# Two-layer transformer on one core: keys stored without zero rows, 64-row score products paired by parity, and loops written out

## The chip, the cores and the metric

One core of one Trainium2 chip runs the whole program. The time is device time in microseconds of one execution, from three runs; lower is better. The engines are named as in the profile: PE (TensorE matmul), PEld (its weight loads), DVE (VectorE), ACT (ScalarE), POOL (GpSimd) and SP (SyncE, which issues DMAs here).

## What is computed

A batch of 4 sequences of 512 tokens by 256 channels goes through two layers, each an attention and a feed-forward part with a residual and a layer norm behind both.

```python
x = layernorm(x + attn0(x))   # 16 heads of 16, 4 key heads, rotary, band |i-j| <= 64, sink
x = layernorm(x + ffn0(x))    # silu(x Wg sg) * (x Wu su), then Wd sd, int8 weights, 1024 wide
x = layernorm(x + attn1(x))   # 16 heads of 16, rotary, causal, biases
x = layernorm(x + ffn1(x))    # shared experts plus the 2 best of 16 experts for each token
```

Both attentions are softmax(q k^T / 4) v for each head:

```python
att = einsum('bhqd,bhkd->bhqk', q, k) * hd ** -0.5    # masked
out = einsum('bhqk,bhkd->bhqd', softmax(att), v)
```

## The kernel before, in words

**Phase 1** handles one sequence of the batch at a time: `batch(b, last)` does attention 0, feed-forward 0 and attention 1, on every engine. Sequences 0 to 2 are turns of a loop (`Fori(0, B - 1)`) and sequence 3 (`last`) stands behind it as straight code. **Phase 2** does the expert layer for all tokens: 4 turns of a loop over the shared experts (`Fori(0, B)`), then 47 tiles of 128 gathered tokens through `run_steps`, in which 7 steps are straight code (`PEELED`), 40 are 5 turns of a loop of 8 steps, and 3 more close it. A step transposes one tile (L1530), multiplies an earlier one with its expert's first weights (L1539), transposes the result of one before that (L1547) and multiplies with the second weights (L1556). The expert of a tile is read into a register (L1510).

**Attention.** A head has 16 channels. For a product of float32 quality q and k are stacked in 48 rows of high and low parts, with row 48 for a shift: 64 rows (`STACK`) for a head, two heads in 128 partitions. `stack` makes them in `q_st` and `k_st` (ACT the high parts, DVE the low), `stack_tr` turns them on PE (L1229, L1238), and copies put them into `qT` and `kT`. `qT` holds an even head in partitions 0 to 63 and the odd one beside it in 64 to 127. `kT` has one block of 128 partitions for every head, of which the other head's 64 rows are zero: a memset at the start (L820) zeroes it, DVE's `k_copy` (L882) fills the even blocks' upper half and ACT (L661) the odd blocks' lower half. So every product uses all 128 rows, and the other head's rows of q meet zeros.

The heads go in 4 groups of 4. A group takes three passes, and six **steps** s = 0 to 5 overlap them: step s does the raw products of group s and the scores, exponentials and value products of group s - 2.

- A **raw item** (`raw_item`) is a query tile t with some heads: a mask product on PE (L1283 in layer 0, L1286 in layer 1), then q times k for each head (L1290) into banks 0 to 2; DVE takes the maximum over the keys (L982) as the shift of the softmax. Layer 0 has 8 items of 2 heads in a step; layer 1 has 11 (one of 4 heads, two of 2, eight of 1). A mask product waits until DVE has read the item three before it.
- A **score item** (`score_item`) is a head with one or two key tiles, k times q (L1303) into banks 3 to 5, which ACT exponentiates (L714, L717) and POOL masks (L518). There are 8 of them in a step in layer 0 and 12 in layer 1.
- `pv_part` multiplies with v (L1317), four heads beside each other in four strips of 32 columns of the array.

PE's order in a step is score item i, then raw item i. All orders are the order of the code; semaphores join the engines. In a loop a wait counts against a register made from the turn (`REGISTER_ALU` rows below). `keep_clock` puts idle products (L1179) where PE would wait.

## Time and profile before

| | |
|---|---|
| median of 3 runs | 1138.18 us |
| lowest, highest | 1136.27, 1138.29 us |
| the profiled execution | 1141.58 us |
| its span, first to last instruction | 1139.9 us |
| mean granted TensorE clock | 0.839 |
| PE, DVE, ACT, POOL busy | 846.4, 628.6, 461.8, 370.5 us |
| phase 1, phase 2 (about) | 0 to 838 us, 838 to 1140 us |

The profile gives start and length of every instruction in us from the span's start. On PE the starts are what to go by: the lengths overlap, since matmuls are pipelined. "idle" in square brackets is what the engine stood still before a row, with what ended it; "issue" means that nothing in the profile was waited for.

### The profile page before, as it was taken

To read this page: it belongs to the slowest core of one execution; us is meant where nothing else is said; L and a number is where in the kernel's file an instruction comes from. 1 tells how busy PE (TensorE), PEld (TensorE's weight loads), DVE (VectorE), ACT (ScalarE), POOL (GpSimd) and SP (SyncE) were. 2 spreads that over 40 slices of the span, in tenths; PEclk is the share of its full clock that TensorE was granted. 3 is DMA by queue.
4 is the path that set the end of the run, shared out by engine and by line. 5 is a ranking of instruction groups with operands and counts; after the bars stand their busy time and mean duration, and the time that the engine had idled before them with its cause. 6 is when DMAs were issued, how large, how long until landed. Compare 5 with 4: busy or idle time off the path is not lost.

```text
span 1139.9 us, 17645 instructions
## 1 busy us (share of the span) xinstructions
PE 846.4 (74%) x5446; PEld 646.4 (57%) x5447; DVE 628.6 (55%) x1478; ACT 461.8 (41%) x960; POOL 370.5 (32%) x595
## 2 busy tenths in 40 slices
PE   2497989988888995878899797889820388889600
PEld 1475765667566664757666575765520277777500
DVE  4473478446248745724884653578360055666555
ACT  1554434744543474454347463444510033444300
POOL 5034441412444041244414142431223600122384
PEclk9598979958888998889899897989855588899955
DMA  9300000000000000000000000000069301243233
GB/s 317 115 3 1 20 1 1 2 20 4 1 20 1 1 2 22 3 1 20 1 1 2 20 2 1 1 1 2 1 206 261 150 18 37 84 126 123 88 111 105
DMA packets 34606, 54.04 MB, mean 47 GB/s; under 512 B 4545, under 2 KB 28865, under 8 KB 33657
## 3 DMA queue, kind: packets, MB, share of 16 engines
q0 software_dynamic: 8192, 27.43, 7.7%
q1 hardware_dynamic: 18624, 18.62, 5.9%
q10 hardware_dynamic: 7704, 6.91, 1.9%
q8 instruction: 46, 0.75, 0.3%
q14 instruction: 40, 0.32, 0.1%
HBM read 24.76 MB, written 20.71 MB: 40 GB/s over the span
## 4 chain that ended last, share of the span: by engine, by line
PE 39%; issue 30%; POOL 13%; DVE 10%; ACT 3%; DMA 2%; another core or an unknown queue 1%; POOLq 0%; SPq 0%; DVEq 0%; ACTq 0%
POOL prob L518 5%; PE ps L1303 4%; PE ps L1194 4%; PE ps L1539 4%; PE ps L1317 3%; PE ps L1179 3%; DVE negmax L982 3%; POOL fT L528 3%; PE ps L1290 3%; PE ps L1556 2%; PE ps L1466 2%; POOL back L576 2%; PE ps L1229 2%; DMA x<-in_x 2%; PE ps L1422 2%
## 5 line engine op out<-in xcount | busy, mean ns | idle before, releaser
L982 DVE TENSOR_REDUCE negmax<-ps 128x2 fp32r<-128x512 f32 (+4 forms) x304 | 178.1, 628 | 61.5 <-PE ps L1290 58.8
L1290 PE MATMUL ps<-kT,qT 128*128 128x256 f32 (+4 forms) x512 | 155.3, 382 | 0.0
L1303 PE MATMUL ps<-qT,kT 128*128 128x192 f32 (+4 forms) x512 | 120.6, 322 | 11.9 <-DVE xT L833 5.1
L513 POOL TENSOR_TENSOR carry_p<-neg_half 128x1 f32<-128x1 f32 x80 | 16.5, 207 | 307.6 <-ACT prob L717 161.9
L518 POOL TENSOR_SCALAR_AFFINE_SELECT prob<-prob 128x512 f32<-128x512 f32 (+1 forms) x192 | 109.9, 602 | 0.0
L1303 PEld LDWEIGHTS ps<-qT,kT 128*128 128x128 f32 x512 | 80.1, 191 | 49.0 <-ACT prob L717 24.2
L616 ACT ACTIVATE xT<-ps 128x256 fp32r<-128x256 f32 x100 | 37.3, 383 | 169.4 <-PE ps L1187 168.7
L717 ACT ACTIVATE prob<-ps 128x512 f32<-128x512 f32 (+1 forms) x192 | 89.2, 518 | 37.6 <-PE ps L1303 36.5
L1290 PEld LDWEIGHTS ps<-kT,qT 128*128 128x128 f32 x512 | 99.0, 207 | 3.3
L1317 PE MATMUL ps<-prob,v_aug 128*32 128x256 f32 (+4 forms) x1024 | 77.9, 412 | 13.2 <-POOL prob L518 13.1
L833 DVE TENSOR_TENSOR xT<-ps,xT 128x256 fp32r<-128x256 f32 x100 | 41.3, 421 | 63.7 <-ACT xT L616 63.4
L714 ACT ACTIVATE prob<-ps,sink 128x448 f32<-128x448 f32 x128 | 71.7, 623 | 11.3 <-PE ps L1303 11.3
L493 POOL TENSOR_TENSOR rstd<-mv,neg_half 128x1 f32<-128x1 f32 x48 | 31.6, 657 | 134.0 <-DVE mv L920 134.0
L557 POOL DMA_DIRECT2D slot_y<-ys_sb x47 | 25.5, 543 | 142.8 <-DVE ys_sb L1135 142.5
L1229 PE MATMUL ps<-ident_r,q_st 128*128 128x128 f32 x256 | 46.8, 339 | 29.8 <-DVE q_st L865 17.9
L968 DVE RECIPROCAL rden<-ps 128x16 f32<-128x16 f32 x32 | 8.2, 255 | 108.4 <-PE ps L1328 108.4
L1229 PEld LDWEIGHTS ps<-ident_r,q_st 128*128 128x128 f32 x256 | 42.3, 246 | 37.9 <-DVE q_st L865 14.8
L1283 PE MATMUL ps<-band,ident_b 128*128 128x384 bf16 (+1 forms) x128 | 50.7, 396 | 16.6 <-issue 9.1
L1187 PE MATMUL ps<-ident,x 128*128 128x128 f32 x136 | 28.8, 312 | 45.1 <-DVE x L938 23.9
L1194 PE MATMUL ps<-wqkv_s,xT 128*128 128x512 f32 (+2 forms) x288 | 59.0, 356 | 2.0 <-ACT qkv_sb L630 1.4
L476 POOL TENSOR_TENSOR rot_c<-qkv_sb,rot 128x320 f32<-128x320 f32 (+1 forms) x32 | 37.3, 1167 | 58.1 <-DVE qkv_sb L949 40.4
L528 POOL TENSOR_TENSOR fT<-fuse_sb,fT 128x512 fp32r<-128x512 f32 x32 | 41.1, 1290 | 45.7 <-ACT fT L742 45.7
(180 smaller groups left out, 1852.9 us busy)
## 6 DMA issues: line engine op xcount, KB each, us to landing
slot_x<-zeros ACTq DMA_DIRECT2D x1, 6016.0 KB, 30.5
xs_sb<-slot_x SPq DMA_DIRECT2D x47, 128.0 KB, 2.0
slot_y<-ys_sb POOLq DMA_DIRECT2D x47, 128.0 KB, 2.0
w_sb<-in_w POOLq DMA_DIRECT2D x4, 1408.0 KB
w_sb<-in_w POOLq DMA_DIRECT2D x5, 704.0 KB, 7.9
x<-in_x SPq DMA_DIRECT2D x4, 512.0 KB, 3.6
x_rows<-x SPq DMA_DIRECT2D x4, 512.0 KB, 3.2
x_all<-x_rows SPq DMA_DIRECT2D x1, 2048.0 KB, 30.4
```

The lines of the kernel that those rows point to most:

```text
L518: ins = pool.affine_select(out=sel, in_=sel, compare_op=ALU.is_ge, fill=0.0, base=base, pattern=[[0, GH], [sign, hi_q - lo_q]], channel_mu ...
L528: pool.tensor_tensor(out=fT[:, 1, m, :], in0=fuse_sb[:, m % 2, :], in1=fT[:, 0, m, :].bitcast(F32), op=ALU.subtract).then_inc(f_lo.sem, 1)
L714: act.activation(prob[:, part % PROB_BUFS, j, 0:n], ps[:, 3 + i % 3, 0:n], ACT.Exp, bias=sink4[:, h:h + 1], scale=SCALE).then_inc(exped[l] ...
L717: act.activation(prob[:, part % PROB_BUFS, j, 0:n], ps[:, 3 + i % 3, 0:n], ACT.Exp, scale=SCALE).then_inc(exped[l].sem, 1)
L982: dve.tensor_reduce(out=negmax[:, t, s * GH + j * mh:s * GH + (j + 1) * mh], in_=ps[:, k % 3, 0:mh * n].rearrange("p (h n) -> p h n", n=n) ...
L1194: ins = pe.matmul(dst, xT[:, a, k, t * P:(t + 1) * P], w[:, w_part, k, c0:c0 + n], start=(i + k == 0), stop=(i == 2 and k == KC - 1))
L1229: ins = pe.matmul(ps[:, 2 + n // 4, (n % 4) * P:(n % 4 + 1) * P], q_st[:, 2 * n:2 * n + 2, :].rearrange("p h s -> p (h s)"), ident_r[:], s ...
L1283: pe.matmul(dst, ident_b[:], band[:, m0:m0 + n].unsqueeze(1).to_broadcast([P, mh, n]), start=True, stop=False, skip_group_check=True)
L1290: ins = pe.matmul(dst[:, jj, :], qT[:, h // 2, t * P:(t + 1) * P], kT[:, k_block(h), k0:k0 + n], start=False, stop=True, skip_group_check= ...
L1303: ins = pe.matmul(ps[:, 3 + item % 3, col:col + n], kT[:, k_block(h), kt * P:(kt + 1) * P], qT[:, h // 2, q0:q0 + n], start=True, stop=Tru ...
L1317: ins = pe.matmul(ps[32 * j:32 * j + 32, 6, q0:q0 + n], v_aug[l][:, kt, h // 4 if l == 0 else h, :], prob[:, (g * n_parts + p) % PROB_BUFS ...
L1539: ins = pe.matmul(ps[:, (r - 1) % 2, 0:2 * I], xsT[:, (r - 1) % 2, part, k, :], w13_sb[:, bass.ds(e, 1), k, :], start=(part + k == 0), sto ...
```

## The change

`kT` loses its zero rows: it has 8 blocks instead of 16, the even head in rows 0 to 63, the odd one in 64 to 127, as `qT`. The memset and all of DVE's `k_copy` go; ACT's copy takes all 128 partitions. A raw or score product now takes the 64 rows of its head (`half(h)`); in the built program these are in 64x128 tiles of the array, at row 0 or row 64, while the mask products, the turning products and the transposes keep the full 128x128 array. A raw item has two heads of the same parity, (1,3) then (0,2), or a single one in the order 1, 0, 3, 2, so that layer 1 has 12 items of one or two heads where it had 11; its neighbouring score item has the other parity. In a step that has both, PE's order becomes mask, raw, score, raw, score. All seven loops on each engine are written out as Python loops.

```diff
+def raw_heads(layer, t):
+    if 2 * query_tile_keys(layer, t)[1] <= 512:
+        return [(1, 3), (0, 2)]
+    return [(1,), (0,), (3,), (2,)]
...
-        kT = sb("kT", [P, H, T], F32R)
+        kT = sb("kT", [P, PAIRS, T], F32R)
...
-    with eng.Fori(0, STEP_TURNS) as m:
+    for m in range(STEP_TURNS):
...
-            with pe.Fori(0, B - 1) as b:
+            for b in range(B - 1):
                 batch(b, False)
...
-                act.activation(kT[STACK:P, 1:2 * n_blk:2, t * P:(t + 1) * P],
-                               ps[STACK:P, K_BANK[l]:K_BANK[l] + 2, :]
+                act.activation(kT[:, 0:n_blk, t * P:(t + 1) * P],
+                               ps[:, K_BANK[l]:K_BANK[l] + 2, :]
...
-            dve.memset(kT[:].bitcast(F32), 0.0).then_inc(start_dve.sem, 1)
...
-            def k_copy(b, l, t):
-                n_blk = (KVH0, PAIRS)[l]
-                dve.wait_ge(*k_tr[l].at(b, t + 1))
-                dve.tensor_copy(kT[0:STACK, 0:2 * n_blk:2, t * P:(t + 1) * P],
...
+                    def half(h):
+                        return slice(STACK * (h % 2), STACK * (h % 2) + STACK)
...
-                            ins = pe.matmul(dst[:, jj, :], qT[:, h // 2, t * P:(t + 1) * P], kT[:, k_block(h), k0:k0 + n],
+                        ins = pe.matmul(raw_dst(g, i)[:, a, :], qT[half(h), h // 2, t * P:(t + 1) * P],
+                                        kT[half(h), k_block(h), k0:k0 + n], start=False, stop=True, skip_group_check=True)
...
-                        for i in range(max(n_items, n_parts * GH)):
-                            if g >= 0 and i < n_parts * GH:
-                                score_item(g, i)
-                            if s < NG and i < n_items:
-                                raw_item(s, i)
+                        for i in range(n_items):
+                            if raws:
+                                raw_mask(s, i)
+                            if scores:
+                                score_free(g, i)
+                            for a in range(2):
+                                if a < raws:
+                                    raw_head(s, i, a)
+                                if a < scores:
+                                    score_tile(g, i, a)
```

How PE's order moves in step 2 of layer 1's attention, items 2 to 4 (L1286 is the mask product, L1290 a raw product, L1303 a score product). Before:

```order
L1303 MATMUL ps<-qT,kT 128x512
L1276 REGISTER_ALU
L1286 MATMUL ps<-causal_q,ident_b 128x128
L1290 MATMUL ps<-kT,qT 128x384
L1300 REGISTER_ALU
L1303 MATMUL ps<-qT,kT 128x384
L1303 MATMUL ps<-qT,kT 128x128
```

The same place in the changed kernel (L1284 mask, L1292 raw, L1310 score, L1350 the turning of the maxima):

```order
L1284 MATMUL ps<-causal_q,ident_b 128x2x128
L1292 MATMUL ps<-kT,qT 128x256
L1310 MATMUL ps<-qT,kT 128x512
L1292 MATMUL ps<-kT,qT 128x256
L1284 MATMUL ps<-causal_q,ident_b 128x128
L1292 MATMUL ps<-kT,qT 128x384
L1310 MATMUL ps<-qT,kT 128x384
L1310 MATMUL ps<-qT,kT 128x128
```

The score now follows a raw product of the other half instead of leading the item, and the register rows are gone.

PE in the expert steps, at the head of a turn of the loop before (L1510 reads the experts, ISA rows put the address into the matmul):

```order
L1510 TENSOR_LOAD owner
L1510 ISA x2
L1534 REGISTER_ALU
L1536 REGISTER_ALU
L1539 ISA
L1539 MATMUL ps<-w13_sb,xsT 128x352
L1539 ISA
L1539 MATMUL ps<-w13_sb,xsT 128x352 x3
L1545 REGISTER_ALU
L1547 MATMUL ps<-ident,h_sb 88x128 x2
L1510 ISA
L1510 TENSOR_LOAD owner
```

In the changed kernel all 40 steps have this form, which is also that of the later straight steps before:

```order
L1524 TENSOR_LOAD owner
L1524 ISA x2
L1553 ISA
L1553 MATMUL ps<-w13_sb,xsT 128x352
L1553 ISA
L1553 MATMUL ps<-w13_sb,xsT 128x352 x3
L1561 MATMUL ps<-ident,h_sb 88x128 x2
L1570 ISA
L1570 MATMUL ps<-w2_sb,hT 128x256
```

The second read of an expert, which the first two steps of every turn had, and the register rows are gone.

## Rows read from the trace of the kernel before

**Rows 1.** The page: the span, and the chain that ended last by engine.

```profile
span 1139.9 us, 17645 instructions
PE 39%; issue 30%; POOL 13%; DVE 10%; ACT 3%; DMA 2%; another core or an unknown queue 1%; POOLq 0%; SPq 0%; DVEq 0%; ACTq 0%
```

**Rows 2.** Windows on single steps: length, busy us and instructions by engine, clock, DMA.

```profile
core 0: us, PE busy (x) PEld busy (x) DVE busy (x) ACT busy (x) POOL busy (x), PEclk, DMA share, GB/s
469.90:475.60 5.70, 5.70 (x44) 5.28 (x45) 4.16 (x7) 4.48 (x9) 1.43 (x4) 1.00 0.01 3
475.60:483.80 8.20, 8.20 (x81) 6.51 (x80) 5.26 (x10) 5.95 (x12) 5.51 (x12) 1.00 0.01 3
...
582.50:588.30 5.80, 5.39 (x31) 3.22 (x32) 5.80 (x11) 0.59 (x1) 0.00 (x0) 1.00 0.01 4
588.30:596.40 8.10, 8.07 (x56) 5.40 (x55) 7.21 (x13) 5.47 (x12) 2.15 (x5) 1.00 0.00 1
596.40:607.10 10.70, 10.59 (x86) 6.74 (x84) 6.90 (x11) 6.76 (x15) 2.92 (x7) 1.00 0.01 2
```

**Rows 3.** Timeline of PE, layer 0: items in steps 3 and 0, and around `pv_part`.

```profile
475.87 0.34 PE L1283 MATMUL ps<-band,ident_b 128*128 128x384 bf16 x1
...
476.50 0.34 PE L1283 MATMUL ps<-band,ident_b 128*128 128x384 bf16 x1
...
476.76 0.27 PE L1290 MATMUL ps<-kT,qT 128*128 128x192 f32 x1
476.96 0.37 PE L1317 MATMUL ps<-prob,v_aug 128*32 128x192 f32 x4
...
477.53 0.39 PE L1317 MATMUL ps<-prob,v_aug 128*32 128x256 f32 x3
477.86 0.36 PE L1303 MATMUL ps<-qT,kT 128*128 128x192 f32 x1
...
651.42 0.39 PE L1283 MATMUL ps<-band,ident_b 128*128 128x512 bf16 x1
...
651.89 0.39 PE L1283 MATMUL ps<-band,ident_b 128*128 128x512 bf16 x1
```

**Rows 4.** Windows on step 0 of layer 0 in sequences 2 and 3.

```profile
455.45:463.69 8.24, 6.08 (x28) 5.05 (x29) 4.49 (x8) 0.02 (x1) 0.00 (x0) 0.59 0.02 5
...
650.21:654.46 4.25, 4.19 (x29) 3.49 (x29) 3.69 (x7) 0.02 (x1) 0.00 (x0) 1.00 0.00 0
```

**Rows 5.** Timeline of PE where sequences 1, 2 and 3 begin.

```profile
256.78 0.48 PE L1283 MATMUL ps<-band,ident_b 128*128 128x384 bf16 x1 [1.68 <-issue]
...
265.25 0.33 PE L1283 MATMUL ps<-band,ident_b 128*128 128x384 bf16 x1
...
455.45 0.32 PE L1283 MATMUL ps<-band,ident_b 128*128 128x384 bf16 x1 [3.82 <-issue]
...
458.68 0.61 PE L1283 MATMUL ps<-band,ident_b 128*128 128x512 bf16 x1 [2.15 <-issue]
...
650.21 0.32 PE L1283 MATMUL ps<-band,ident_b 128*128 128x384 bf16 x1 [0.60 <-ACT kT L661]
```

**Rows 6.** Timeline of PE in the expert steps, straight and looped.

```profile
983.58 0.38 PE L1530 MATMUL ps<-ident,xs_sb 128*128 128x128 f32 x2
...
986.87 0.38 PE L1530 MATMUL ps<-ident,xs_sb 128*128 128x128 f32 x2
...
1007.43 0.91 PE L1539 MATMUL ps<-w_sb,xsT 128*128 x4 [0.68 <-issue]
...
1024.44 0.91 PE L1539 MATMUL ps<-w_sb,xsT 128*128 x4 [0.71 <-issue]
```

**Rows 7.** Timeline of PE and DVE around the last `stack_tr` of sequence 3.

```profile
647.20 1.08 PE L1229 MATMUL ps<-ident_r,q_st 128*128 128x128 f32 x8 [1.00 <-ACT qT L657]
...
648.77 0.68 DVE L882 CAST kT<-ps 64x512 fp32r<-64x512 f32 x1 [1.52 <-PE ps L1238]
```

**Rows 8.** Timeline of ACT in the first turn of the shared experts.

```profile
901.94 0.32 ACT L786 ACTIVATE act_a<-ps 128x176 f32<-128x176 f32 x1 [7.37 <-issue]
```

More of the change, by code:

```diff
@@ L407, in _ @@
                 load(q, q)
-            with sp.Fori(0, (NS - 4) // 4) as m:
+            for m in range((NS - 4) // 4):
                 for r in range(4):
@@ L533, in _ @@
                 head_step(0, k)
-            with pool.Fori(0, B - 1) as b:
+            for b in range(B - 1):
                 batch(b, False)
@@ L560, in _ @@
                 store(q, q)
-            with pool.Fori(0, (NS - 3) // 4) as m:
+            for m in range((NS - 3) // 4):
                 for i in range(4):
@@ L762, in _ @@
             act.activation(gw_s[:, 0, :, :], gw_raw[:], ACT.Copy).then_inc(gw_split.sem, 1)
-            with act.Fori(0, B - 1) as b:
+            for b in range(B - 1):
                 batch(b, False)
@@ L774, in _ @@
             load_table(2, ACT.Silu)
-            with act.Fori(0, B) as b:
+            for b in range(B):
                 for t in range(NT):
@@ L931, in norm @@
                             split_lo(b, ("x1", "x2")[i], t)
-                    if i == 2 and not last:
-                        k_copy(b + 1, 0, NT - 1)
                 def scale_tile(i, t, result):
@@ L1025, in _ @@
                               op=ALU.subtract).then_inc(gw_split.sem, 1)
-            with dve.Fori(0, B - 1) as b:
+            for b in range(B - 1):
                 batch(b, False)
@@ L1090, in _ @@
             dve.wait_ge(x3_back.sem, 16)
-            with dve.Fori(0, B) as b:
+            for b in range(B):
                 for t in range(NT):
@@ L1434, in _ @@
             pe.wait_ge(gw_split.sem, 2)
[L1435 removed]
+            for b in range(B - 1):
                 batch(b, False)
@@ L1450, in _ @@
             pe.wait_ge(shared_in.sem, 32)
-            with pe.Fori(0, B) as b:
+            for b in range(B):
                 pe.wait_ge(*xg_in.at(b, 16))
```

89 lines of the change are left out of this document (44 added, 45 removed).

## The prediction

> **What bounds the kernel now.** I first read the page's chain. Its largest share after PE is "issue", time in which an engine waited for nothing that the profile shows, a third of it [rows 1]. So the question is what PE does where it is the last to come, and two places matter here: the scoring steps of both attentions, which are about 100 of the 200 us of a sequence, and the expert steps of phase 2.
>
> Second, windows cut at the first product of a step. Steps with scores and raws are long and PE is busy all through them ([rows 2], the first two and the last two), with DVE and ACT at 5 to 7 us of the same window. In layer 1 a step with raw products alone takes 5.80 us, and DVE's 11 maxima fill all of it ([rows 2], third): there PE may be slower without anyone noticing, up to a point. In layer 0 such a step takes 4.25 us at the full clock ([rows 4], second).
>
> Third, the timeline of PE gives what one item costs. A raw item of 512 mask columns and two products of 256 takes 0.47 us from mask to mask ([rows 3], last two), 0.61 ns for a column. An item with scores in layer 0 takes 0.63 us from mask to mask ([rows 3], first two): 384 mask columns, 0.16 us at 2.4 columns a ns, and four products in the other 0.47 us, so 0.12 us each.
>
> Fourth, the places where a loop turns [rows 5, 6].
>
> **The loops written out.** *Expert steps.* A row that comes once in a turn of 8 steps comes again after 17.01 us ([rows 6], last two); I looked at four such rows and they are all 17.0 us apart. In front of it PE stands for 0.7 us with nothing to wait for. The straight steps ahead of the loop, which already carry all four stages, take (986.87 - 983.58) / 2 = 1.645 us ([rows 6], first two). The order of the changed kernel shows the 40 looped steps in just that form: no register arithmetic, no second read of an expert. 8 x 1.645 = 13.2 us for a turn, so 3.85 us less, and 5 x 3.85 = **-19.3 us**. What could come late then: SP's loads and POOL's stores, one each for a step; in the straight steps they kept up. Bounds: 0 if the straight steps owe their speed to loads that were made ahead, -21 if all goes as in the best of them.
>
> *Between sequences.* Sequence 3 follows without a jump: PE starts it 0.60 us after its idle products, when ACT's copy is there, and has done step 0 after 4.25 us. Sequence 2 starts after 3.82 us for no reason shown, stands again for 2.15 us, falls to a mean granted clock of 0.59 and needs 8.24 us for the same step [rows 4, 5]. That is 3.2 + 4.0 = 7.2 us. Sequence 1: 1.68 - 0.60 = 1.1 us and 265.25 - 256.78 - 4.25 = 4.2 us, together 5.3. The stops look like code that has to be read again after the jump. Sum **-12.5 us**; the lower bound, if the clock stays low there anyway, is the stops alone, about -7.
>
> *Shared experts.* Their turns follow each other through data, so I take nothing. There is one unknown: in the first turn ACT stands for 7.37 us with nothing to wait for [rows 8], while the experts' weights come in. The same code is read there after the change. It may go either way by a few us; I take 0.
>
> **The copies.** DVE loses `k_copy`, 0.68 us in layer 0 [rows 7]. But PE's start of the next turning product waits for ACT's copy of q, and DVE stands for 1.52 us before its copy [rows 7]: ACT's copies and PE's products are the loop there, and ACT's copy keeps its length, for it has the same columns in more partitions. The memset at the start lies under the first loads. I take **0**; the bound is one copy a sequence, -3 us in all.
>
> **The scoring steps.** No 64-row tile is in the trace. The nearest is the one other place where PE changes the shape of its tiles, from 128x128 to strips of 128x32 and back [rows 3]. From the last full product to the first strip it is 0.20 us where products otherwise follow after 0.12: 0.08 us of standstill. And the first product behind a change is 0.36 us long where its like is 0.27: 0.09 us, in which its weights are loaded, that are otherwise loaded under the product before. So a change costs up to 0.17 us. The changed kernel changes twice for each raw item, since masks stay at 128 rows and the products are at 64. For the way back, to the mask, whose bf16 weights load faster, I take half of the second part less: 0.26 us an item in all, between 0 (rows of a tile may change freely) and 0.34.
>
> The page "TensorEngine Tiling (Array Packing)" of the Trainium skill says in its section "Key Properties" that a change of the tiling mode, not of the tile alone, drains TensorE. By that rule each mask of this kernel costs two drains; the rows on the strips agree with it, and no row here shows it for a change of rows.
>
> Against that stands the pairing. A raw product and the score behind it are in different halves, write different banks, and may run together. The four strip products start within 0.02 us of each other: 0.37 us for four [rows 3]. So for a pair I take one product's time.
>
> - Layer 0, step 0: 8 raw items of 0.42 us (0.47 and, by the same ns a column, 0.35 to 0.37 for the narrow ones) plus 0.26: 5.4 us against 4.25, **+1.2**. Step 1 has 6.2 us of other work on DVE, and hides it: 0.
> - Layer 0, steps 2 and 3: per item + 0.26 - 2 x 0.12 = 0.02, so +0.15 a step, **+0.3**.
> - Layer 1, steps 0 and 1: by 0.61 ns a column the 12 items are 2 x 0.31 + 2 x 0.47 + 4 x 0.31 + 4 x 0.39 = 4.4 us, plus 12 x 0.26 = 3.1: 7.5 us against 5.80, so DVE's cover is gone, +1.7 each, **+3.4**. DVE's twelfth maximum is covered then.
> - Layer 1, steps 2 and 3: + 3.1 us of changes, less what pairs hide: 0.21 for a 512-column score under the two raws of an item, 0.16 for 384 columns, 0.12 for 256, four items each, 2.0 us. PE has +1.1 us, of which I let half go into the waits for ACT and DVE that these steps have: **+1.1** for both. Bounds: 0 and 2.2.
> - Steps 4 and 5 have no masks, change no more often than before, and are ACT's: 0.
>
> Sum 6.0 us a sequence, **+24 us**. A hundredth of a us in the cost of an item is some 0.6 us a sequence where PE leads, so 2.4 us in all.
>
> Last, the new order puts a mask's wait for DVE ahead of the score that stood before it. Queued behind it are the score, and with it ACT. With three banks ahead this seldom binds in steps 2 and 3, where DVE is busy 7 of 8 to 10 us; I take 0, and at most 0.2 us a step.
>
> **Sum.** 1138.2 - 19.3 - 12.5 + 24.0 = **1130 us**. On the profiled execution, 1141.58 us with a span of 1139.9, the same terms give 1133.8; it lies 3.4 us above the median of the runs.
>
> **Rivals.**
> (a) *Changing rows is free and pairs overlap.* Then steps 0 and 1 stay DVE's, step 2 of layer 0 ACT's, and the gain is in step 3 of layer 0, 8 x 0.24 = 1.9 us of which 1.5 count, and in steps 2 and 3 of layer 1, 2.0 us of work each of which 0.5 and 1.5 count: 3.5 us a sequence, -14. 1138.2 - 31.8 - 14 = **1092 us**. For it speaks that the rows on the change are of columns, not of rows; against it, that both directions of that change cost. The Trainium skill's page "TensorE: Matmul & The Clock Gate", section "Part 3: Packing small matmuls", has row tiles run side by side, four of them 3.07 times as fast as one after another; no row here shows it.
> (b) *Free, but the pairs don't overlap*: the scoring stays, **1106 us**.
> (c) *Slower: the changes cost and the pairs don't overlap*, because the weights of a pair are loaded one after another. A product of 192 columns needs 0.08 us at 2.4 columns a ns but takes 0.12, so loading bounds layer 0's items already. Then steps 2 and 3 cost 8 x 0.26 = 2.1 us each in layer 0, and 3.1 less 1 us of waits in layer 1: 1.2 + 4.2 + 3.4 + 4.2 = 13 us a sequence, +52: **1158 us**. In general the kernel gets slower when the scoring costs over 8 us a sequence, that is at 0.29 us an item by my sum.
> (d) *Writing out the expert loop gives nothing*, as code must be brought for every step: -19.3 is gone, **1150 us**. Against it stand the straight steps.
>
> **How the numbers follow.** Forecast 0.43, (a) 0.22, (b) 0.10, (c) 0.18, (d) 0.07. The forecast's own range, by 0.20 to 0.31 us an item, is 1115 to 1143; two thirds of it are below 1136. The range goes to (a), and towards (c) without reaching it: 1093 to 1153. A measurement of this kernel can tell about 0.2% from no change. Faster: 0.22 + 0.10 + 0.29 = 0.61; same: 0.08; slower: 0.31.
>
> **What would show it.** In the expert steps the transposes (L1530 before) must come 1.6 to 1.7 us apart throughout. Sequences 1 and 2 must start like sequence 3, without "issue" of 2 to 4 us. In layer 1 step 0, the window must grow from 5.80 to about 7.5 us with DVE no longer busy throughout, and the first raw product behind a mask must start 0.1 us or more after the mask's columns are through; if it starts 0.04 us behind the mask as before and the window stays at 5.8, (a) or (b) holds. Whether a raw product and the score behind it start within 0.02 us of each other tells (a) and the forecast from (b) and (c). My sum is wrong from the ground if the first turn of the shared experts grows or shrinks by over 10 us, or if the clock in the scoring steps falls with the standstills.

## The result, and the profile after

| | before | after |
|---|---|---|
| median | 1137.22 us (1134.86 to 1138.29) | 1269.76 us (1261.04 to 1276.79) |
| span of the profiled execution | 1139.9 us | 1264.2 us |
| mean granted TensorE clock | 0.839 | 0.734 |

The changed kernel takes 1.1165 times as long (95% interval 1.1085 to 1.1244): 132 us slower, where 8 us less was forecast, and far beyond the range of 1093 to 1153 us.

The page of the changed kernel; the rows that answer to [rows 1], and the granted clock in 40 slices of the span (tenths):

```profile
span 1264.2 us, 15264 instructions
...
PEclk9556976687678757978875896697576565789955
...
PE 68%; DVE 10%; ACT 5%; POOL 5%; DMA 5%; issue 4%; another core or an unknown queue 2%; ACTq 0%; DVEq 0%; SPq 0%; POOLq 0%
```

"issue" fell from 30% to 4% of the chain, and PE took its place and more. It is 4% too in the kernel with the loops alone written out (below), which gains 1%: a large share of the chain under "issue" was not time to be won.

Windows on the steps of sequence 2, cut at the first product of a step: steps 0 to 3 of layer 1, then steps 0 to 3 of layer 0. The columns are those of [rows 2]; the last but two is the granted clock.

```profile
core 0: us, PE busy (x) PEld busy (x) DVE busy (x) ACT busy (x) POOL busy (x), PEclk, DMA share, GB/s
646.05:653.55 7.50, 7.50 (x29) 3.88 (x27) 6.16 (x11) 0.00 (x0) 0.00 (x0) 0.90 0.00 0
653.55:665.08 11.53, 11.53 (x33) 5.88 (x32) 7.23 (x12) 0.59 (x1) 0.00 (x0) 0.50 0.00 1
665.08:679.14 14.06, 14.06 (x57) 6.95 (x56) 7.22 (x12) 6.29 (x12) 2.14 (x5) 0.50 0.01 2
679.14:696.65 17.51, 17.51 (x85) 8.55 (x86) 7.00 (x12) 7.27 (x14) 2.91 (x7) 0.50 0.01 1
517.75:523.88 6.13, 6.13 (x29) 3.51 (x28) 4.91 (x8) 0.13 (x1) 0.00 (x0) 1.00 0.01 3
523.88:531.47 7.59, 6.54 (x34) 3.75 (x32) 6.34 (x13) 1.86 (x5) 0.00 (x0) 1.00 0.00 1
531.47:540.70 9.23, 9.23 (x45) 4.82 (x44) 4.45 (x8) 5.00 (x8) 2.32 (x5) 0.56 0.00 1
540.70:551.39 10.69, 10.69 (x82) 5.52 (x82) 5.55 (x10) 6.53 (x11) 4.63 (x10) 0.74 0.01 2
```

This is the whole finding in eight rows. Layer 1's steps 1, 2 and 3 took 5.80, 8.10 and 10.70 us at 1.00 before [rows 2], and step 0 took 5.80 us as well:

```profile
576.70:582.50 5.80, 5.30 (x28) 2.87 (x26) 4.99 (x10) 0.00 (x0) 0.00 (x0) 1.00 0.00 0
```

After, step 0 takes 7.50 us and is nearly through when the clock drops; steps 1 to 3 run at 0.50, that is at 1.2 instead of 2.4 GHz, and PE is busy all through them. DVE and ACT, with 7 us of work each, are no bound any more. In layer 0 the clock holds for two steps and drops in the third.

Timeline of PE in layer 0: an item of step 0, then a paired item of step 3, both at the full clock.

```profile
518.28 0.34 PE L1281 MATMUL ps<-band,ident_b 128*128 128x384 bf16 x1
518.54 0.47 PE L1292 MATMUL ps<-kT,qT 64*128 64x192 f32 x2
518.94 0.39 PE L1281 MATMUL ps<-band,ident_b 128*128 128x512 bf16 x1
...
549.35 0.34 PE L1281 MATMUL ps<-band,ident_b 128*128 128x384 bf16 x1
549.62 0.35 PE L1292 MATMUL ps<-kT,qT 64*128 64x192 f32 x1
549.62 0.38 PE L1310 MATMUL ps<-qT,kT 64*128 64x256 f32 x1
...
550.02 0.34 PE L1281 MATMUL ps<-band,ident_b 128*128 128x384 bf16 x1
```

A raw product and its score start together (549.62 twice), so pairs overlap. The first raw product starts 0.26 to 0.27 us behind a mask whose 384 columns need 0.16 us, so 0.10 us is a standstill; the rest of what the item grew by stands between its products and the next mask. An item takes 0.67 us where it took 0.63 [rows 3].

Two neighbouring expert steps, and the longest stop of ACT in the first turn of the shared experts (the places of [rows 6, 8]):

```profile
1139.79 0.38 PE L1544 MATMUL ps<-ident,xs_sb 128*128 128x128 f32 x2
...
1141.45 0.38 PE L1544 MATMUL ps<-ident,xs_sb 128*128 128x128 f32 x2
...
1054.94 0.32 ACT L791 ACTIVATE act_a<-ps 128x176 f32<-128x176 f32 x1 [12.22 <-remote]
```

Put together from the two traces, span against span (+124.3 us): the scoring of layer 0, from the first mask product to the last transpose of a sequence, went from 188.5 to 243.0 us over the four sequences, +54.5; layer 1's from 209.7 to 301.0, +91.3; the rest of phase 1 is 16.2 us shorter; the routing and the end give 5.5 us back; the shared experts went from 87.2 to 102.5, +15.3; the expert steps from 95.4 to 80.3, -15.1.

### The profile page after: what moved, and what is told of

Same layout as the page of the kernel before. It is cut to its first block, busy times and chain, and to the rows that moved or that the text cites. A ratio compares the mean times of both kernels' runs of the same rounds, so it can differ in the third digit from the quotient of the medians.

```text
span 1264.2 us, 15264 instructions
## 1 busy us (share of the span) xinstructions
PE 991.3 (78%) x5462; PEld 668.5 (53%) x5462; DVE 608.4 (48%) x1461; ACT 468.0 (37%) x960; POOL 367.8 (29%) x595
## 4 chain that ended last, share of the span: by engine, by line
PE 68%; DVE 10%; ACT 5%; POOL 5%; DMA 5%; issue 4%; another core or an unknown queue 2%; ACTq 0%; DVEq 0%; SPq 0%; POOLq 0%
PE ps L1292 13%; PE ps L1325 7%; PE ps L1428 5%; PE ps L1310 5%; PE ps L1184 4%; PE ps L1281 4%; PE ps L1284 4%; DMA xg<-x_rows 4%; PE ps L1169 3%; PE ps L1553 3%; PE ps L1219 3%; PE ps L1177 3%; POOL back L582 2%; PE ps L1480 2%
## 5 line engine op out<-in xcount | busy, mean ns | idle before, releaser
L974 DVE TENSOR_REDUCE negmax<-ps 128x2 fp32r<-128x512 f32 (+4 forms) x320 | 193.5, 610 | 186.2 <-PE ps L1292 181.6
L1292 PE MATMUL ps<-kT,qT 64*128 64x256 f32 (+4 forms) x512 | 212.2, 483 | 0.0
L1310 PE MATMUL ps<-qT,kT 64*128 64x256 f32 (+4 forms) x512 | 168.1, 466 | 6.3 <-ACT prob L720 4.9
L1292 PEld LDWEIGHTS ps<-kT,qT 64*128 64x128 f32 x512 | 114.3, 261 | 66.2 <-issue 49.1
L723 ACT ACTIVATE prob<-ps 128x512 f32<-128x512 f32 (+1 forms) x192 | 94.2, 522 | 97.1 <-PE ps L1310 96.5
L1325 PE MATMUL ps<-prob,v_aug 128*32 128x256 f32 (+4 forms) x1024 | 108.7, 549 | 9.7 <-POOL prob L524 9.6
L1310 PEld LDWEIGHTS ps<-qT,kT 64*128 64x128 f32 x512 | 95.0, 259 | 38.4 <-ACT prob L723 14.1
L1281 PE MATMUL ps<-band,ident_b 128*128 128x384 bf16 (+1 forms) x128 | 59.8, 467 | 10.2 <-DVE gw_s L1014 5.2
L1284 PE MATMUL ps<-causal_q,ident_b 128*128 128x128 bf16 (+1 forms) x192 | 59.3, 309 | 0.0
L1325 PEld LDWEIGHTS ps<-prob,v_aug 128*32 128x32 f32 x1024 | 31.0, 135 | 49.8 <-issue 26.1
```

The source lines that it names most:

```text
L723: act.activation(prob[:, part % PROB_BUFS, j, 0:n], ps[:, 3 + i % 3, 0:n], ACT.Exp, scale=SCALE).then_inc(exped[l].sem, 1)
L974: dve.tensor_reduce(out=negmax[:, t, s * GH + heads[0]:s * GH + heads[-1] + 1:2], in_=ps[:, k % 3, 0:mh * n].rearrange("p (h n) -> p h n", ...
L1281: pe.matmul(dst, ident_b[:], band[:, m0:m0 + n].unsqueeze(1).to_broadcast([P, mh, n]), start=True, stop=False, skip_group_check=True)
L1284: pe.matmul(dst[:, :, n - P:n], ident_b[:], causal_q[:].unsqueeze(1).to_broadcast([P, mh, P]), start=True, stop=False, skip_group_check=True)
L1292: ins = pe.matmul(raw_dst(g, i)[:, a, :], qT[half(h), h // 2, t * P:(t + 1) * P], kT[half(h), k_block(h), k0:k0 + n], start=False, stop=Tr ...
L1310: ins = pe.matmul(ps[:, 3 + item % 3, col:col + n], kT[half(h), k_block(h), kt * P:(kt + 1) * P], qT[half(h), h // 2, q0:q0 + n], start=Tr ...
```

## The experiments

All times come with the ratio to the kernel before on the same chip. The kernels on one line of thought stand together.

| kernel | median us | ratio to before (95%) |
|---|---|---|
| only the loops written out | 1129.8 | 0.9907 (0.9863 to 0.9952) |
| changed kernel, but full rows | 1109.3 | 0.9726 (0.9701 to 0.9751) |
| the same, shared experts a loop again | 1098.5 | 0.9654 (0.9605 to 0.9703) |
| changed kernel, pairs taken apart | 1401.6 | 1.2146 (1.2054 to 1.2238) |
| changed kernel without masks | 1130.7 | 0.9921 (0.9873 to 0.9969) |
| full rows without masks | 1111.2 | 0.9784 (0.9718 to 0.9851) |
| full rows, masks in column strips | 1240.0 (1201.7 to 1246.9) | no interval |
| changed kernel, masks twice | 1260.3 (1237.2 to 1278.6) | no interval |
| masks twice in layer 0, four times in layer 1 | 1255.0 | 1.0997 (1.0899 to 1.1094) |

The kernels with stops inside their items have wide times, since layer 0 of one and the same code is found at either level of the clock (below). Their medians are read loosely, and their steps closely. The traces read are of one execution each: 1415.8 us of the kernel with pairs taken apart, 1242.3 with strips (the fastest took 1201.7), 1257.4 with masks twice, and 1294.7 with masks two and four times, the longest of its five.

### Which part of the change costs

**Only the loops.** The kernel before with `for ... in range` for every `Fori`.

> The kernel before with all its loops written out and nothing else changed. By my sum the expert steps give 19.3 us and the starts of sequences 1 and 2 give 12.5 us: 1137 - 32 = 1105 us. Two readings differ. (1) The written-out loops are good by themselves and all of the loss is in the scoring: 1105 us, each sequence about 200 us, shared experts 141 us as before. (2) The written-out code costs something where the changed kernel lost 22 us in the shared experts: then this kernel shows 160 us there too, and about 1125 us in all. In both the granted clock is 1.00 in the scoring steps of layer 1.

Measured 1129.8 us: a gain of 1%, some 10 us, a third of the 32 us. The clock stayed at 1.00 in layer 1's scoring and the steps kept their length. The expert steps took 79.8 instead of 95.4 us (-15.6), the routing begins 8 us earlier, but the shared experts took 99.5 instead of 87.2 us. Reading (2).

**Full rows.** The changed kernel with this taken back, and with it the memset, DVE's copies and the numbering of the blocks:

```diff
-        kT = sb("kT", [P, PAIRS, T], F32R)
+        kT = sb("kT", [P, H, T], F32R)
...
-qT[half(h), h // 2, t * P:(t + 1) * P], kT[half(h), k_block(h), k0:k0 + n]
+qT[:, h // 2, t * P:(t + 1) * P], kT[:, k_block(h), k0:k0 + n]
```

> The changed kernel with one thing taken back: keys keep their zero rows, so that raw and score products use the full 128x128 array (with DVE's copies and the memset that belong to it). The new order mask, raw, score, raw, score, the items of one parity, the twelfth item of layer 1 and the written-out loops stay. (Half) If the 64-row tiles are the cause, by their effect on the clock or by their switches, the granted clock stays 1.00 in the scoring steps, and the time is that of the kernel with only the loops written out, within 6 us. (Order) If the new order is the cause, in which a mask's wait for DVE stands ahead of the score and so ahead of ACT, PE shows stops before the masks and the time stays over 1200 us.

Measured 1109.3 us. The clock is back, with the new order, the twelve items and the loops in place (layer 1 of sequence 2, steps 2 and 3):

```profile
567.70:575.50 7.80, 7.80 (x56) 5.44 (x56) 6.69 (x13) 5.56 (x12) 2.15 (x5) 1.00 0.02 4
575.50:585.45 9.95, 9.95 (x86) 6.63 (x85) 6.74 (x13) 6.78 (x15) 2.92 (x7) 1.00 0.01 2
```

So the 64-row tiles cost 160 us, and the order costs nothing. It even gains: this kernel is 20 us below the one with loops alone, outside the 6 us that I had allowed. These two steps took 8.20 and 10.60 us there, 0.40 and 0.65 us more. Between the two traces, whose executions are 12.8 us apart, the scorings of all sequences are 11.7 us shorter; 2.8 us of that are step 0 of layer 0, which was entered at a higher clock. Where the rest of the 20 us comes from is not settled.

**Pairs taken apart.** The changed kernel with the score item ahead of the mask:

```diff
-                            for a in range(2):
-                                if a < raws:
-                                    raw_head(s, i, a)
-                                if a < scores:
-                                    score_tile(g, i, a)
+                            for a in range(scores): score_tile(g, i, a)
+                            raw_mask(s, i)
+                            for a in range(raws): raw_head(s, i, a)
```

> The changed kernel with 64-row products, but in the old order: both products of a score item, then the mask, then both raw products, so that neighbouring products are hardly ever in opposite halves. Two switches of the tile shape for each raw item stay. It tells what the pairing gives. The changed kernel hides one product of 0.12 us (0.2 at half clock) behind another for each pair: 16 pairs a step in layer 0, 16 to 24 in layer 1. If the pairs were worth their full time, this kernel takes 8 x 2 x 0.12 to 0.2 = 2 to 3 us more in each of the four steps with raws and scores, 8 to 12 us a sequence and 32 to 48 us in all: 1300 to 1318 us. (Activity) If the clock follows how busy the array is, the standstills in a longer step lower it further or no less, and layer 1 stays at 0.50. (Pairs worthless) the same 1270 us.

Measured 1401.6 us, 132 us above the changed kernel, three times what I expected. At half the clock every product that isn't hidden counts double: steps 2 and 3 of layer 1, at 0.50 in both kernels, took 18.56 and 22.7 us instead of 14.06 and 17.51. In layer 0 the same two steps took 13.7 us and some 16 at 0.50, where those of the changed kernel took 10.0 and some 12 when they ran at 0.50. That is about 17 us a sequence, some 70 us in all, for the pairing. Another 30 us are not the pairing's: layer 0 ran at the lower level from its step 0 on (10.4 us instead of 6.1, and 12.7 instead of 7.6). The pairing works, as forecast; it cannot pay for what makes it possible.

### Standstills or half rows

**Masks left out.** Both kernels leave out the mask products of the raw items; the maxima then cover masked keys too.

> The changed kernel without its mask products (the first raw product starts the bank instead; the maxima then cover masked keys too, which the output doesn't show where no exponential underflows). So the scoring steps have 64-row products, pairs and all, but no change of the tile shape inside an item; what changes is left to the value products and the transposes of the shifts. It is to be read against the same kernel with full rows, which has no masks either. (Standstills) If the clock falls because of the stops at the changes of shape, it stays at 1.00 here in layer 1's scoring, and pairing can pay for the first time: layer 0 steps 2 and 3 and layer 1 steps 2 and 3 get shorter than with full rows by some 2 x 0.8 and 2 x 1 us, and the time is at or below that of the full-row kernel without masks, about 1070 to 1095 us. (Half rows) If 64-row products count for less in what grants the clock, it still falls to 0.50 here, and the time stays above 1150 us.

> The full-row kernel in the new order (1109 us) without its mask products: the control for the 64-row kernel without them. The masks of steps 2 and 3 are 3584 columns a step in layer 0, 1.5 us, and 2048 in layer 1, 0.85 us; in steps 0 and 1 DVE bounds. Up to 2 x 1.5 + 2 x 0.85 = 4.7 us a sequence, 19 in all: 1090 us, or more where ACT bounds step 2. No theory has the clock fall here, unless it is less work alone that lowers it.

Steps 1 and 2 of layer 1 in sequence 2, with half rows, then with full rows:

```profile
571.50:578.70 7.20, 6.57 (x20) 4.03 (x21) 6.43 (x13) 0.59 (x1) 0.00 (x0) 0.53 0.00 1
578.70:587.80 9.10, 9.01 (x47) 5.83 (x47) 6.53 (x12) 5.47 (x11) 2.15 (x5) 0.50 0.00 1
```

```profile
552.50:558.75 6.25, 5.40 (x21) 2.85 (x21) 6.25 (x13) 0.59 (x1) 0.00 (x0) 0.97 0.00 1
558.75:568.50 9.75, 9.75 (x44) 7.89 (x45) 6.92 (x13) 5.83 (x12) 2.15 (x5) 0.67 0.01 2
```

Without a change of shape inside an item most of the loss is gone (1270 to 1131 us), yet the clock still falls in these steps with half rows. So "standstills alone" falls. So does "the time stays above 1150". Half rows still cost 20 us here (1131 against 1111). The full-row kernel without masks is no faster than with them (1111 against 1109 us), where 1090 was expected: its clock falls too in places, 0.67 in step 2, where it was 1.00 with masks. So the masks were work that kept the clock up. That it falls because PE now waits for DVE (PE is busy 5.40 of 6.25 us in step 1) is likely and not shown.

**Strips.** The full-row kernel with each mask in four column strips, which changes the tile shape twice for an item, with no half row:

```diff
-                            pe.matmul(dst, ident_b[:], band[...], start=True, stop=False)
+                        for j in range(4):
+                            pe.matmul(dst[32 * j:32 * j + 32], ident_b[:, 32 * j:32 * j + 32], band[...], start=True, stop=False)
```

> The full-row kernel in the new order (1109 us) with each mask product made as four products of 128x32 in the four column strips: all products have 128 rows, and the tile shape changes twice for each raw item, as in the changed kernel. In the probe a full product of 256 columns in front of strips took 0.318 us and the strips 0.222 us, where products in one shape take 0.120: 0.30 us for the two changes. (Standstills) The granted clock falls to 0.50 in layer 1's scoring, as in the changed kernel, and the time is 1270 us or more, since nothing is paired: up to the 1400 us of the unpaired 64-row kernel. (Half rows) Without half rows the clock stays at 1.00; the changes cost 0.3 us an item alone, at most 8 x 4 and 12 x 4 items a sequence, 24 us less what DVE's share of steps 0 and 1 covers, some 18 us a sequence, 72 in all: 1180 us.

Steps 2 and 3 of layer 1 in sequence 2, and the stretch ahead of layer 0 and its step 0:

```profile
662.15:672.70 10.55, 10.55 (x96) 6.43 (x92) 7.28 (x14) 6.37 (x13) 2.15 (x5) 1.00 0.00 2
672.70:684.70 12.00, 12.00 (x120) 7.41 (x117) 6.87 (x12) 7.19 (x14) 2.92 (x7) 1.00 0.01 2
...
495.00:507.70 12.70, 12.10 (x49) 8.93 (x50) 5.22 (x15) 7.13 (x12) 1.19 (x2) 0.50 0.12 41
507.70:518.10 10.40, 10.40 (x57) 5.58 (x53) 5.39 (x9) 0.76 (x2) 0.00 (x0) 0.50 0.01 2
```

Each theory is half right. In layer 1 the stops stretch the steps (12.00 us against 9.95), but the clock stays at 1.00: stops without half rows don't lower it. Layer 0 is entered at 0.50 and stays there for three steps, 35.6 us, in every sequence. The full-row kernel without strips is entered at 0.50 as well and is at once back:

```profile
430.00:440.50 10.50, 9.90 (x38) 7.35 (x39) 4.97 (x14) 6.44 (x11) 0.65 (x1) 0.50 0.14 50
440.50:444.90 4.40, 4.34 (x29) 3.64 (x28) 3.68 (x7) 0.01 (x1) 0.00 (x0) 0.96 0.02 4
```

**Probes** behind PE's last expert product. Their blocks are plain loops of products of 256 columns, for instance D and H:

```python
pe.matmul(ps[:, 1, 0:256], full, moving)            # D: full, half, full, ...
pe.matmul(ps[:, 0, 0:256], half, moving_half)
...
pe.matmul(ps[:, 0, 0:128], ident_b, idle_b[:, 0:128])   # H: full mask, two half products
pe.matmul(ps[:, 0, a * 256:(a + 1) * 256], half, moving_half)
```

> The kernel before with written-out loops; behind PE's last expert product, while the other engines finish, PE runs seven blocks of idle products whose results nobody reads, each behind 60 idle products of 128x512 that should bring the clock to its upper level. The time is not to be compared. Blocks: A 160 full-array products of 256 columns; B 200 of 64 rows in one half; C 300 of 64 rows in alternating halves and banks; D 100 pairs of a full and a 64-row one; E 64 groups of a full one and four strips of 128x32; F 40 items of a 512-column mask and four 64-row products in alternating halves, as in the changed kernel; G the same items with full rows. (Rows count) If a 64-row product counts for less with whatever grants the clock, B falls to 0.50 although no tile shape changes in it, F falls, and D lies between; A, E, G stay at 1.00. (Standstills) If it is the standstills at switches, D, E and F fall, and A, B, C and G stay. Times at the full clock: A and B 0.107 us a product, C 0.055 if halves run beside each other and weights load in time, up to 0.12 if not; D 0.107 + 0.107 + 0.2 of switches; F 0.65 us an item against 0.64 in G.

Windows of the first probe: B, C, D without its first 6 us (in which it is still at 1.00), E, F. G, the items of F with full rows, stays at 1.00 too.

```profile
1141.10:1165.30 24.20, 24.20 (x201) 24.07 (x202) 0.00 (x0) 0.00 (x0) 0.00 (x0) 1.00 0.00 1
1178.40:1196.50 18.10, 18.10 (x300) 17.97 (x301) 0.00 (x0) 0.00 (x0) 0.00 (x0) 1.00 0.01 2
...
1216.00:1307.80 91.80, 91.80 (x181) 51.48 (x182) 0.00 (x0) 0.00 (x0) 0.00 (x0) 0.50 0.00 0
1322.00:1356.60 34.60, 34.60 (x322) 18.38 (x322) 0.00 (x0) 0.00 (x0) 0.00 (x0) 1.00 0.00 1
1369.60:1399.70 30.10, 29.09 (x198) 15.66 (x201) 0.00 (x0) 0.00 (x0) 0.00 (x0) 1.00 0.00 1
```

B takes 24.2 / 200 = 0.121 us a product and C 18.1 / 300 = 0.060: halves run beside each other at full value. Only D falls, about 6 us after it began, and stays down to its end. E has stops and full rows and stays up. F, with masks of 512 columns, stays up too: I had expected it to fall. A, full products behind the expert steps and 60 idle products, was at 0.50 for 31 of its 46 us and came back while it ran.

> Five blocks of idle products behind the last expert product, each behind 80 idle products of 128x512, as in the first probe, on the kernel before with written-out loops. The time is not to be compared. B2: 400 products of 64 rows and 256 columns in one half; C2: 700 in alternating halves; H: 80 items of a 128-column mask of the full array and two 64-row products, as in layer 1's steps 0 and 1 of the changed kernel; J: 80 items with the mask in four column strips and two full products, so the same two changes of shape without a half row; M: 80 items with a full mask and two full products, no change of shape. (Both are needed) B2 and C2, half rows without a standstill, stay at 1.00, about 0.120 and 0.060 us a product; J, standstills without half rows, stays at 1.00; H falls to 0.50; M stays. (Half rows alone) B2 falls as well. (Standstills alone) J falls as well. An item of H and of J should take some 0.5 us at the full clock, one of M some 0.33.

Windows of the second probe: C2, H without its first 4 us, J (B2 is below). M, whose items take 0.36 us, stays at 1.00 too. Then the masks of two neighbouring items of H and of J in the timeline.

```profile
1192.60:1234.60 42.00, 42.00 (x701) 42.00 (x700) 0.00 (x0) 0.00 (x0) 0.00 (x0) 1.00 0.01 2
...
1257.00:1325.00 68.00, 68.00 (x218) 43.58 (x217) 0.00 (x0) 0.00 (x0) 0.00 (x0) 0.50 0.00 0
1345.40:1393.40 48.00, 48.00 (x480) 31.85 (x480) 0.00 (x0) 0.00 (x0) 0.00 (x0) 1.00 0.00 1
```

```profile
1254.39 0.23 PE L1578 MATMUL ps<-idle_b,ident_b 128*128 128x128 bf16 x1
...
1254.98 0.23 PE L1578 MATMUL ps<-idle_b,ident_b 128*128 128x128 bf16 x1
...
1350.19 0.24 PE L1584 MATMUL ps<-idle_b,ident_b 128*32 128x128 bf16 x4
...
1350.79 0.24 PE L1584 MATMUL ps<-idle_b,ident_b 128*32 128x128 bf16 x4
```

H and J are the cleanest pair. An item takes 0.59 us in H and 0.60 in J, with the same columns and nearly the same stops. What differs is where the shape changes: J splits the mask's columns and keeps all rows, H halves the rows of the products. H falls after 4 us while J stays at 1.00 for 48 us. With C2, half rows without a change, also at 1.00, both are needed. B2 seems not to fit: its 64-row products fell to 0.50 after some 5 us and stayed there to their end.

> The two probes disagree on half rows without a standstill: 200 products of 64 rows stayed at 1.00 in the first, 400 fell to 0.50 after some 5 us in the second and stayed there to their end; the full products at the same place in the first probe fell too, but came back to 1.00 while they ran. Here, behind 240 idle products, four blocks of 300 products of 256 columns, one behind the other in one tile shape: half rows, full rows, half rows, full rows, each followed by 120 idle products, and last 100 items of a full mask and two 64-row products. The time is not to be compared. (Half rows alone are enough) Both half-row blocks fall and stay at 0.50 to their end, both full-row blocks stay at 1.00 or come back. (Marginal) The two half-row blocks differ. (Place) Only the first block falls, whatever it is, since the fall comes from what precedes it. The last block falls as it did in the second probe.

Windows of the third probe: the first two blocks, half and full rows, and the mixed block without its first 4 us. The other two blocks read as these two, 1.00 and 36 us each.

```profile
1088.40:1124.30 35.90, 35.90 (x300) 35.90 (x300) 3.10 (x10) 0.00 (x0) 0.93 (x1) 1.00 0.09 31
1150.30:1186.30 36.00, 36.00 (x302) 35.97 (x300) 0.00 (x0) 0.00 (x0) 0.00 (x0) 1.00 0.00 1
...
1342.00:1427.90 85.90, 85.90 (x274) 55.01 (x273) 0.00 (x0) 0.00 (x0) 0.00 (x0) 0.50 0.00 0
```

Half rows without a stop hold the clock in both blocks; the mixed block falls again. So the fall of B2 came from its place behind the expert steps, as A's did. The timeline shows what happened there: PE stood between products, for nothing that the profile shows. These are two rows of B2, then one of A.

```profile
1092.64 1.08 PE L1572 MATMUL ps<-xsT 64*128 64x256 f32 x3 [0.65 <-issue]
...
1107.10 66.27 PE L1572 MATMUL ps<-xsT 64*128 64x256 f32 x309 [0.41 <-issue]
...
1119.66 8.50 PE L1572 MATMUL ps<-xsT 128*128 128x256 f32 x58 [0.61 <-issue]
```

B2 has such stops of 0.2 to 0.7 us from 1086 us on, and its clock fell at 1088; A has them, up to 0.9 us, from 1087 to 1120, and fell at 1092. The third probe's blocks begin when the other engines are nearly through, and have none. Why PE stood is not shown; in A and B2 DVE, POOL and the transfers were still at work. What comes after is the clearest row on half rows: from 1107.10 on B2 ran 309 products without a stop, 0.21 us each, and stayed at 0.50 for all of the 66 us, while A was back at 1.00 soon after its own stops ended.

### More work, shorter steps

The changed kernel with each mask product issued twice; in a second kernel the last line of the edit says 4, for layer 1.

```diff
+                            for _ in range(2):
                                 pe.matmul(dst, ident_b[:], band[...], start=True, stop=False)
...
+                            for _ in range(2):
                                 pe.matmul(dst[:, :, n - P:n], ident_b[:], causal_q[...], start=True, stop=False)
```

> The changed kernel (1270 us) with each mask product issued twice, one behind the other; the second starts the bank anew, so nothing else changes. That is more work of the full array and not one more change of the tile shape: 3584 columns a step in layer 0 and 2048 in layer 1, 1.5 and 0.85 us at 2.4 GHz and twice that at 1.2. (Clock) If the time was lost to the clock, and the clock falls because 64-row products with standstills between them are too little work, more work raises it: steps 1 to 3 of layer 1 go back from 11.5, 14.1 and 17.2 us at 0.50 towards 8, 11 and 13 us at 1.00, and the kernel gets faster although it does more, by up to 40 us: 1230 us. (Time alone) If the clock doesn't follow, the second masks cost 4 x 3.0 us in layer 0 and 3 x 1.7 us in layer 1 at the half clock, 17 us a sequence, and the time is about 1330 us.

> The changed kernel with each mask product issued twice in layer 0 and four times in layer 1, nothing else changed. With masks twice in both layers the clock was 1.00 in steps 0 to 3 of layer 0 in sequences 1 to 3, but still 0.50 in steps 1 and 2 of layer 1. (Clock) With the added work of full rows the clock stays at 1.00 in layer 1 as well. Each step of layer 1 then has 3 x 2048 columns more than the changed kernel, 2.6 us at 2.4 GHz, and still steps 1 to 3 shrink from 11.5, 14.1 and 17.2 us to about 10.6, 11.3 and 13 us; with the steps all at one clock it can be read what the changes of shape cost by themselves: this step less the added masks less the same step of the full-row kernel (5.6, 6.2, 7.9 and 9.9 us). I expect 2, 1.8, 0.8 and 0.5 us in layer 1. The time is about 1235 us. (Otherwise) If the clock of layer 1 stays at 0.50, the steps grow by 5 us each and the time is over 1300 us.

Layer 0 of sequence 2 with masks twice (steps 0 and 3), and layer 1 with masks four times (steps 1, 2 and 3), then step 0 of layer 0 of that second kernel:

```profile
519.80:527.50 7.70, 7.70 (x38) 3.75 (x37) 5.02 (x9) 0.45 (x2) 0.00 (x0) 1.00 0.00 0
...
544.10:553.50 9.40, 9.40 (x87) 4.64 (x86) 5.10 (x9) 6.21 (x11) 4.63 (x10) 1.00 0.00 1
```

```profile
690.10:699.90 9.80, 9.80 (x69) 5.88 (x68) 7.21 (x13) 0.59 (x1) 0.00 (x0) 1.00 0.00 1
699.90:711.10 11.20, 11.20 (x93) 6.53 (x92) 7.21 (x13) 6.67 (x13) 2.15 (x5) 1.00 0.01 2
711.10:723.65 12.55, 12.55 (x117) 7.31 (x117) 6.54 (x12) 6.88 (x13) 2.92 (x7) 1.00 0.01 2
...
533.00:546.40 13.40, 13.40 (x37) 5.92 (x36) 5.53 (x10) 0.77 (x2) 0.00 (x0) 0.50 0.00 1
```

With 2.56 us more of masks in each step, steps 1 to 3 of layer 1 take 9.80, 11.20 and 12.55 us where the changed kernel took 11.53, 14.06 and 17.51: the clock is the cause, shown by the edit that moves it. Twice the masks were not enough in layer 1: there steps 1 and 2 stayed at 0.50 and grew to 13.2 and 15.8 us, a miss, and only step 3 got shorter. The medians gained 10 and 15 us, less than the 35 to 40 expected, and as whole kernels neither is clear of the changed kernel's scatter. The same code of layer 0 took 7.70 us for step 0 in the first kernel, entered at 1.00, and 13.40 us in the second, entered at 0.50, where the level stayed for three steps. Inside one execution of the first kernel, too, steps 0 and 1 took 13.3 and 15.0 us in sequence 0, and 7.7 and 9.1 in the others. That goes with the scatter of these kernels' times.

### The loop put back

The full-row kernel with `Fori(0, B)` again for the four turns of the shared experts.

> The full-row kernel in the new order (1109 us) with one loop put back: the four turns over the shared experts in phase 2 are a loop again on SP, ACT, DVE and PE; all other loops stay written out. In the kernels with all loops written out the first of these turns took 47.7 to 49.5 us, in the kernel before 37.9. (Code) If it is the written-out code, which ACT must read while the expert weights come in, the first turn goes back to some 38 us, and the time to about 1100 us, if the three jumps back cost less than 1 us each. (Other) If the turn is longer for another reason, an earlier start of phase 2 or the transfers, it stays at 48 us and the time at 1109 us, or above it by the jumps.

Measured 1098.5 us, the fastest kernel of the study; the ratio is 0.7% below that of the full-row kernel, about 8 us, with intervals that just touch. The first turn took 42.4 us instead of 47.7 (48.1 and 48.5 in the two kernels without masks, on the same chip), though not the 37.9 of the kernel before: about half of the effect goes with the written-out code. But that code alone does not make the turn long. The third probe has the very code of the kernel with loops alone up to its last expert product, and ran on another chip, on which the kernel before took 1116.4 us. There this turn took 17.6 us and ACT had no stop in it, against 46 to 50 us in every other trace with the loops written out. What the stops hang on is open, and so is whether the 8 us hold on such a chip.

## Why the prediction was wrong, by its own steps

**The step that failed** is one that the sum took for granted: every duration was taken at a granted clock of 1.00. The prediction named "the clock in the scoring steps falls with the standstills" as what would make the sum wrong from the ground, and gave it neither a chance nor a price. Both were to be had. [rows 4] shows step 0 at 0.59 taking 8.24 us (2.15 of them a stop) and 4.25 at 1.00; and at the lower level the 5.80, 8.10 and 10.70 us of [rows 2] take up to twice as long, up to 24.6 us a sequence and 98 us in all for three steps of layer 1 alone. That was a rival of its own, with a longer time than (c). The runs showed it: 0.50 in steps 1 to 3 of layer 1 and in parts of layer 0.

**The scoring's +24 us** came out in sum, for a good part by luck. With the full clock held by added masks, and those masks taken off (an estimate: 1.49 us a step in layer 0, 2.56 in layer 1), steps 0 to 3 take 6.2, 7.6, 6.0 and 7.9 us in layer 0, +3.4 against before (step 0 at its full-clock 4.25), and 7.0, 7.2, 8.6 and 10.0 us in layer 1, +2.5. That is 5.9 us a sequence, forecast 6.0. Its split was off: layer 0 was forecast at 1.5 and layer 1 at 4.5. Layer 0's step 0 was put at 5.4 us and took 6.13, since an item there takes 0.53 us on average, not the 0.42 I used; step 1 was put at nothing and cost 1.4. Layer 1's steps 2 and 3 were put at +1.1 and come out 0.2 below before. Against the full-row kernel in the same order the half rows cost 7.3 us a sequence at the full clock; the new order, put at nothing, gave 1.4 back.

The 7.5 us of layer 1's step 0 were luck too. The 0.61 ns a column is a misreading: that item has 512 mask columns and 512 more in its two products, 1024 in 0.47 us, which is 0.46 ns, and by it the step would be 3.3 + 3.1 = 6.4 us. Its items took 0.53 to 0.65 us at the full clock, about 7.0 us for all; 7.50 were measured because the last two ran at 0.50. The 5.80 us that the forecast set against it are the row of step 1, where DVE is busy throughout; step 0 took 5.80 us as well, with DVE busy for 4.99. The whole scoring grew by 145.8 us, plus the 8.2 us that the better starts of sequences 1 and 2 gave inside it: 154. Less 24, the clock cost about **130 us**, an estimate. The full-row kernel gives the same: its scorings are 160 us shorter, of which 4 x 7.3 are the half rows at the full clock.

**The cost of a change of shape**, 0.26 us an item: (6.13 - 4.25) / 8 = 0.24, and 0.59 in H against 0.36 in M, 0.23. Right.

**Pairs overlap**: right (549.62 twice; 0.060 against 0.121 us in the probe), and some 70 us at the clock that this kernel gets. The Trainium skill's page "TensorE: Matmul & The Clock Gate", section "Part 3: Packing small matmuls", has row tiles run side by side; for two halves the probe agrees with it, a factor of 2.0.

**The expert steps**, -19.3: measured -15.1. Six of the 40 steps that were looped still took over 2 us, 3.3 us too much together. The term was a fifth too large. Rival (d) is out.

**Between sequences**, -12.5: step 0 is 6.13 to 6.14 us in sequences 1 to 3 alike, and the stops of 2 to 4 us are gone. The term was too small here: 8.2 us inside the scoring, and the three stretches from one sequence's scoring to the next took 69.5 us before and 58.6 after, together 19 us. It hangs on the clock, though. In the kernel with loops alone steps 0 of sequences 2 and 3 took 5.4 and 5.5 us at a clock of 0.73, and phase 1 gained 8 us.

**The shared experts**, 0: measured +15.3 (+12.3 with the loops alone). It was named as the other thing that would upset the sum, and it took back the gain of the expert steps. The first turn went from 37.9 to 48.7 us, with ACT standing for 10 and 12 us, and the cause is open (above). The Trainium skill's page "Runtime: NRT & Kernel Launch", section "Instruction fetch mechanics", says that a taken branch to a page of code that isn't held costs a fetch, and that crossing into the next block of straight code is mostly hidden. For the stops at the loops' heads the trace agrees; for this turn, 42.4 us as a loop and 47.7 written out, but 17.6 written out on another chip, the runs leave it open.

**Copies**: 0. Against the full-row kernel, which has the copies and the memset, the stretches between the two scorings of a sequence are the same within 0.3 us, and the first scoring begins 1.0 us earlier.

## What to carry to other kernels

Price a change of PE's work twice, at 2.4 and at 1.2 GHz, and give the lower level a chance of its own whenever the change takes work or rows away and adds stops; in this kernel that was some 130 us against 24. Zero rows in a product cost no time here (0.120 us a product with 64 rows or 128), and they kept the clock. Write out loops one by one and measure each by itself: the expert loop gained 15 us, and the shared experts' loop was better left a loop on the chips where that was measured.

## What the runs showed of the hardware

- Of four kinds of work on PE, full rows without stops brought the clock from 0.50 back to 1.00 and held it. Full rows with stops of 0.1 to 0.2 us held 1.00 for 48 us when entered there, but stayed at 0.50 for 35.6 us when entered at 0.50. Half rows without stops did the same: they held 1.00 in five blocks of 18 to 42 us, and stayed at 0.50 for 66 us behind stops. Half rows with stops fell from 1.00 in the probes D, H and the mixed block after 4 to 6 us, and in layer 1's step 0 of the changed kernel. They did not fall in F, nor for two steps of layer 0, 13.7 us, where the masks are three to four times as long as H's.
- A full and a 64-row product of 256 columns in turn take 0.31 us each at the full clock, where they take 0.12 in one shape: 0.19 us for a change between two such products. From a bf16 mask to a 64-row product it is about 0.10 us, and an item with the change there and back takes 0.23 to 0.28 us more. The Trainium skill's page "TensorEngine Tiling (Array Packing)", section "Key Properties", says that a change of mode drains TensorE; these rows agree, also for a change of rows alone, and give it a price.
- The clock in the profile is a record, and twice it was wrong. With pairs taken apart, step 0 of layer 0 took 10.35 us in sequence 0, where the record says 1.00, and 10.40 us in the others at 0.50; with masks twice, sequence 0 has 1.00 beside a step of 13.3 us, which took 13.4 at 0.50 in the kernel with masks two and four times. There the length of a known step is the better witness.
- Leaving out the masks, 3584 and 2048 columns a step, gave the full-row kernel nothing (1111 against 1109 us).
